# Writing out the loops over the groups on ScalarE and VectorE of a four-layer cross-attention kernel

## What is computed

```
x = L0(x, ctx)   # 1x1 convolutions over the 64 rows, both inputs normalised, attention 256 x 256
x = L1(x, ctx)   # 16 heads of 16: layer norm of ctx, Q K V, softmax, output product, times tanh(gate)
x = L2(x, ctx)   # as L1 with its own weights
x = L3(x, ctx)   # one head of 256, softmax over 64 keys, times alpha

def L1(x, ctx):  # L2 is the same
    a = layer_norm(ctx) * gamma + beta
    Q, K, V = heads(x @ Wq.T), heads(a @ Wk.T), heads(a @ Wv.T)
    p = softmax(where(mask, Q @ K.T * 0.25, -inf))
    return x + tanh(gate) * (merge(p @ V) @ Wo.T)
```

## Time and profile before

| | us |
|---|---|
| median of 3 runs | 617.71 (616.09 to 618.76) |
| the profiled execution | 619.04 |
| its span, first to last instruction | 616.9 |
| PE busy in the span | 570.0 (92%) |
| DVE busy, ACT busy | 469.0 (76%), 469.4 (76%) |
| POOL busy | 118.0 (19%) |

### The profile page before, as it was taken

The page is one execution under the profiler, slowest core; times in us unless marked ns, Lnnn a source line. Parts: engine busy times, 40 slices in busy tenths (PEclk is TensorE's granted clock), DMA queues, the critical chain, the costliest instruction groups (busy, mean ns, idle before and its releaser), DMA issues.

```text
span 616.9 us, 25805 instructions
## 1 busy us (share of the span) xinstructions
PE 570.0 (92%) x10867; PEld 502.2 (81%) x10867; DVE 469.0 (76%) x1023; ACT 469.4 (76%) x961; POOL 118.0 (19%) x132
## 2 busy tenths in 40 slices
PE   1799999999999999999999999999999999999885
PEld 1678788888888887988889887998889888998774
DVE  5785879676986879687786869778796869876553
ACT  0799878878787779867788869867788768868651
POOL 3503070103310070102500060101601051000000
PEclk9899999999999999999999999999999999999978
DMA  6420001110020100210020100210020100010001
GB/s 154 161 75 2 2 3 44 35 37 1 3 75 4 34 2 4 74 36 2 2 75 3 36 2 3 74 36 3 2 75 2 37 2 2 3 36 3 3 2 34
DMA packets 18499, 18.32 MB, mean 30 GB/s; under 512 B 1828, under 2 KB 18340, under 8 KB 18404
## 3 DMA queue, kind: packets, MB, share of 16 engines
q1 hardware_dynamic: 18024, 16.55, 8.5%
q0 software_dynamic: 320, 0.26, 0.4%
q10 hardware_dynamic: 60, 0.01, 0.0%
HBM read 12.63 MB, written 4.19 MB: 27 GB/s over the span
## 4 chain that ended last, share of the span: by engine, by line
PE 65%; DVE 15%; ACT 10%; issue 6%; DMA 1%; SPq 1%; POOL 0%; DVEq 0%; ACTq 0%; POOLq 0%
PE psum L389 10%; PE psum L731 8%; PE psum L677 8%; PE psum L391 8%; PE psum L390 8%; DVE negmax L1055 7%; PE psum L724 5%; DVE shifted L1059 4%; PE psum L641 4%; ACT work L856 3%; PE psum L656 3%; PE psum L544 3%; ACT v L807 2%; PE psum L453 2%; DMA mrow_u<-in_mask_dram 1%
## 5 line engine op out<-in xcount | busy, mean ns | idle before, releaser
L1059 DVE TENSOR_TENSOR shifted<-psum,negmax 128x512 f32<-128x512 f32 x128 | 88.5, 692 | 10.5 <-ACT work L856 5.6
L856 ACT ACTIVATE work<-shifted 128x512 f32<-128x512 f32 x128 | 79.1, 631 | 18.8 <-DVE shifted L1059 17.8
L870 ACT ACTIVATE work<-psum,group_mask 128x512 f32<-128x512 f32 x128 | 80.4, 696 | 16.4 <-PE psum L677 16.4
L1055 DVE TENSOR_REDUCE negmax<-psum 128x8 f32<-128x512 f32 x128 | 87.3, 682 | 5.9 <-PE psum L656 5.3
L677 PEld LDWEIGHTS psum<-const,work 64*128 64x128 f32 x1536 | 55.8, 141 | 33.4 <-issue 32.0
L677 PE MATMUL psum<-const,work 64*128 64x64 f32 x1536 | 65.0, 229 | 18.7 <-ACT work L856 16.6
L731 PEld LDWEIGHTS psum<-v,work 128*64 128x64 f32 x2048 | 63.9, 141 | 8.1 <-issue 5.9
L731 PE MATMUL psum<-v,work 128*64 128x34 f32 x2048 | 67.5, 227 | 0.0
L851 ACT ACTIVATE work<-psum,negmax 128x256 f32<-128x256 f32 x128 | 50.2, 511 | 12.2 <-DVE negmax L1051 12.2
L807 ACT ACTIVATE v<-psum 64x256 f32<-64x256 f32 x128 | 49.7, 388 | 10.0 <-PE psum L391 8.7
L795 ACT ACTIVATE kbd<-psum,own_bias,const 128x512 f32<-128x512 f32 x64 | 46.2, 777 | 4.8 <-PE psum L391 4.4
(11 more groups left out here) (181 smaller groups left out, 1536.1 us busy)
## 6 DMA issues: line engine op xcount, KB each, us to landing
x_raw<-in_x_dram SPq DMA_DIRECT2D x8, 512.0 KB, 4.3
c_raw<-in_ctx_dram SPq DMA_DIRECT2D x8, 512.0 KB, 5.0
out_dram<-attn SPq DMA_DIRECT2D x16, 256.0 KB, 2.3
mrow_u<-in_mask_dram SPq DMA_DIRECT2D x8, 64.0 KB, 5.1
kbd<-in_L_xattn_Wq_dram SPq DMA_DIRECT2D x2, 256.0 KB, 6.3
kbd<-in_L_xattn_Wk_dram SPq DMA_DIRECT2D x2, 256.0 KB, 6.5
kbd<-in_L_xattn_Wv_dram SPq DMA_DIRECT2D x2, 256.0 KB, 6.6
kbd<-in_L_xattn_Wo_dram SPq DMA_DIRECT2D x2, 256.0 KB, 7.1
```

The lines of the kernel that those rows point to most:

```text
L856: act.activation(probs[:, exp_row(g, l, i, last), :], shifted[:, i % 2, :], ACT.Exp).then_inc(exps, 1)
L870: act.activation(probsT[:, at, :], o[:], ACT.Copy, scale=group_mask[:, 2 * i + c:2 * i + c + 1]).then_inc(free, 1)
L1055: dve.tensor_reduce(negmax[:, i % 2, :], sv, AX_X, ALU.max, negate=True).then_inc(rowmax, 1)
L1059: dve.tensor_tensor(shifted[:, i % 2, :].rearrange("t (j k) -> t j k", k=C), sv, negmax[:, i % 2, :].unsqueeze(2).broadcast_to([P, NJ, C]) ...
```

## The change

The two loops of the chip become Python loops, so that all seven groups are written out with `g` a number. Nothing else in the file changes.

```diff
@@ scalar
-            with act.Fori(0, NG - 1) as g:
+            for g in range(NG - 1):
                 iteration(g, False)
             iteration(NG - 1, True)
@@ vector
-            with dve.Fori(0, NG - 1) as g:
+            for g in range(NG - 1):
                 iteration(g, False)
             iteration(NG - 1, True)
```

## The result

The changed kernel takes 621.12 us in the median (619.59 to 622.73, 7 runs), the kernel before, timed beside it, 618.45. The ratio is 1.0054 with a 95% interval of 1.0035 to 1.0074: slower by 0.5%, which is 3.3 us; the two medians as they stand differ by 2.7 us. The interval stays clear of 1, but its lower end lies under the 0.5% that the prediction named as the least that can be told. The forecast was 622.6 us, 4.9 us slower. The direction was right and the time lies in the range, but a third of the forecast loss did not come. The profiled execution took 621.38 us, its span is 619.4.

The account below looks back on a forecast made before the run. DVE was taken to set the time in layer 2's scores, though PE is busiest. Terms of 0.28 + 0.28 + 0.14 = 0.70 us a group, 4.9 us over seven, gave 617.7 + 4.9 = 622.6 us; range just under 619.7 to 626.0.

Parts of the forecast that it names:

- S2.0 to S2.3, four gaps: Layer 2's first four reduce-subtraction pairs on DVE: each costs 0.07 us more, all on the path to T2.0, 0.28 us a group.
- S2.4 to S2.7, four gaps: Layer 2's last four pairs on DVE, up to the release of cT.0: another 0.28 us a group.
- AT1.0 and AT1.1: DVE's attnT_lo steps after ACT's attnT_hi: PE's weight load comes 0.07 us later at each, 0.14 us a group.
- ScalarE's waits: On ACT nearly every activation carries its one wait itself in both forms; register instructions run under the activation before: 0 us.
- Mn.0, layer 1's scores, branch, L3, A1.0: Other moved waits and DVE's loop branch: 0 us, being off the path or covered by other work.
- period: The time of one group in the loop: up by 0.28 + 0.28 + 0.14 = 0.70 us.
- the stretch from S1.0 to T1.0 unchanged at 6.6 us: Layer 1's scores: moved waits cost 0 us, as the loop took 6.62 us and the written-out last group 6.61.
- A (absorbed): Layer 2: only the first half's 0.28 us reaches PE, the rest vanishes in PE's work; 619.7 us, chance 0.08.
- C (fetches): Longer DVE and ACT code: about six fetch stops of 1.1 us add 6.6 us; 629 us, chance 0.05.
- D: Nothing on the chip changes, the loop's waits being in truth as slow; 617.7 us, chance 0.03.
- B: Register instructions at L1058 hold up the waits behind them; removing them gains 4.2 us, 613.5 us; chance 0.04.

Follow-up runs that it names:

- e8: The kernel before, both loops kept, with one more POOL instruction of 128 x 200 numbers ahead of the eight normalisations L1282; 617.24 us, ratio 1.0011.
- e5: The kernel before, both loops kept, with rowmax waited for ahead of exps at the scores' subtractions; 615.07 us, ratio 0.9977.
- e9: The kernel before, both loops kept, with rowmax waited for ahead of exps and mask_set ahead of the bank at T1.0; 614.69 us, ratio 0.9961.
- e3: The changed kernel with rowmax waited for ahead of exps at the scores' subtractions (L1059, L1067); 615.12 us, ratio 0.9969 to the kernel before.
- e6: The kernel before, both loops kept, with ACT's mask_set waited for ahead of the bank at T1.0; 616.08 us, ratio 0.9999.
- e4: The changed kernel with DVE's two waits swapped at the scores and at cT/nT, Mn/Mm, AT1, AT2 and the first weighting step; 615.92 us, ratio 0.9972.
- e1: The changed kernel with ACT's loop kept, so only DVE's is written out; 621.25 us against 617.35 for the kernel before, ratio 1.0067.
- e10: The changed kernel with only the attn_hi and bank waits swapped at AT1 and AT2; one profiled execution, S1.0 to S2.0 26.66 us, 0.15 shorter.
- e2: The changed kernel with DVE's loop kept, so only ACT's is written out; 616.97 us, ratio 0.9993 to the kernel before.

## Why L990 gets shorter: e7 and e8

L990 at L.3 reads two tiles from SBUF, and POOL is at its eight normalisations L1282 at that time, one directly behind the other. What stands beside it in the changed kernel and in the kernel before (timelines of POOL and DVE):

```profile
370.63 1.21 POOL L1282 TENSOR_SCALAR x_norm<-x_raw,mean_var,rstd 128x256 f32<-128x256 f32 x1
```

```profile
368.72 1.22 POOL L1282 TENSOR_SCALAR x_norm<-x_raw,mean_var,rstd 128x256 f32<-128x256 f32 x1
```

In the changed kernel L990 starts 371.07 - 370.63 = 0.44 us behind POOL's instruction and takes 0.68. Before, it was 369.02 - 368.72 = 0.30 us and 0.79. To move nothing but this phase, e7 and e8 put one more POOL instruction ahead of the eight, of 128 x 8 numbers in e7 and 128 x 200 in e8, and keep both loops:

```diff
@@ normalise, against the kernel before; e8 has 0:200
                 hold(rstd_ready, nth)
+                pool.tensor_scalar(pool_pad[:, 0:8], x_raw[:, 0, 0:8], EPS, None, ALU.add)
                 for t in list(range(NP, 2 * NP)) + list(range(NP)):
```

> The kernel before with one POOL instruction more ahead of the eight normalisations L1282 (128 x 8 numbers into a scratch, about 0.2 us), so all eight start about 0.2 us later. In six traces VectorE's L990 at L.3 (operands in SBUF alone) lasts 681 ns plus what is missing to 410 ns from the start of the L1282 beside it: 789 to 809 ns in the kernel before, where it starts 281 to 304 ns behind, and 681 to 683 in the changed kernel, where it starts 420 to 434 ns behind. Theory (POOL holds something that L990 needs for the first 0.41 us of each L1282): L990 now starts 50 to 110 ns behind L1282 and lasts 980 to 1040 ns; the stretch from S2.0 to S2.3 grows from 6.10 to 6.30 to 6.35 us, the period by 0.2 to 0.25, the time by 1.4 to 1.7 us. Rival: L990's length has nothing to do with POOL's phase and the shorter L990 of the changed kernel comes from its being written out; then it stays at 790 to 810 ns here.

> The same with a POOL instruction of 128 x 200 numbers, about 1.0 us, ahead of the normalisations. One L1282 takes 1.20 us, so L990 at L.3 now starts about 500 ns behind the start of the L1282 beside it, beyond 410. Theory: L990 lasts 681 to 683 ns as in the changed kernel, though the loop stays, the stretch from S2.0 to S2.3 falls from 6.10 to 5.98 us, the period by about 0.1 us, the time by 0.8 us, within what can't be told. Rival as before: L990 stays at 790 to 810 ns. A second rival is that the later end of the normalisations delays PE's turning of x_norm and the period grows.

Measured: e7 617.62 us, ratio 1.0015 (0.9989 to 1.0040); e8 617.24 us, ratio 1.0011 (0.9984 to 1.0037). Both times are too small a matter to tell; the traces are not. POOL and DVE in e7 (lines are one or two higher there, L991 is the L990 of before):

```profile
370.52 1.22 POOL L1284 TENSOR_SCALAR x_norm<-x_raw,mean_var,rstd 128x256 f32<-128x256 f32 x1
```

```profile
370.62 0.99 DVE L991 TENSOR_TENSOR state_lo<-state,state_hi 128x512 fp32r<-128x512 f32 x1
```

At 0.10 us behind POOL's start the same instruction takes 0.99 us, in all seven groups (991 to 997 ns), and the period grows by 0.18 us, just under the 0.2 to 0.25 expected. That is the length that the theory forecast, with the loop in place; the rival's 790 to 810 ns falls. In e8 the phase did not become the 500 ns that I wanted, but 312 to 327, and the length is 760 to 778 ns: by the same rule (681 + 410 - 326 = 765), though the 681 to 683 ns expected were missed. The added instruction took 0.73 us and not 1.0, and the first L1282 behind it became 0.5 us longer. The second of these shows the reverse side. POOL and DVE in e8, further ahead in the same group:

```profile
361.20 1.71 POOL L1284 TENSOR_SCALAR c_norm<-c_raw,mean_var,rstd 128x256 f32<-128x256 f32 x1
```

```profile
361.12 0.68 DVE L991 TENSOR_TENSOR state_lo<-state,state_hi 128x512 fp32r<-128x512 f32 x1
```

Here L991 started 0.08 us ahead of POOL's instruction; it kept its 0.68 us, and POOL's took 1.71 instead of 1.21. Whoever comes second waits. Over all twelve traces L990 starts 78 times less than 410 ns behind the start of an L1282; start difference and duration then add up to 1085 to 1105 ns each time. In the 83 cases in which it starts later beside a running L1282, it takes 679 to 692 ns.

The Trainium skill, "SBUF — State Buffer", section "Who interferes with whom", says that a VectorE instruction with two SBUF inputs contends with a GpSimd instruction that reads SBUF; section "SBUF: two separate sides" of the same page says that whichever of the two starts first has the ports for its whole instruction and the other is blocked. On who blocks whom the traces agree, in both directions. On how long they don't: by the whole instruction L990 would have to end 1.21 + 0.68 = 1.89 us behind POOL's start, and it ends 1.09 behind it, as if POOL's share in it were over after 0.41 us of the 1.21 that the profile shows for it.

## Are the loops needed away: e5 and e9

e5 is the kernel before with e3's swap and both loops.

```diff
@@ scores_step, layers 1 and 2, against the kernel before (L3 as in e3)
+                    dve.wait_ge(rowmax, 18 * g + (8 * l - 8 + i + 1))
                     if l == 2 or i >= 2:
                         dve.wait_ge(exps, 18 * g + (8 * (l - 1) + i - 1))
-                    dve.wait_ge(rowmax, 18 * g + (8 * l - 8 + i + 1))
```

> The kernel before, loops and all, with only the two waits of L1058 (and those of the third layer at L1066) called in the other order: rowmax first, exps second. In this form a wait instruction holds exps, L1059 holds rowmax, and the register instruction carries no wait. My theory: what counts is only which instruction holds the wait that ends last, so layer 2's pairs stay at a gap of 0.03 us as in the kernel before, the period stays at 70.17 to 70.21 us, and the time is that of the kernel before within 0.3 us (the change as submitted loses, and the same reordering only repairs the written-out form). Pairs of layer 1 that wait for exps (gaps of 0.12 us in the loop, where a register instruction holds it) come to 0.10, on no path. Rival: the gain of the reordered, written-out kernel (615.1 against 617.35) comes from the reordering itself; then this one shows it too, 615 to 616 us.

Measured: 615.07 us, ratio 0.9977 (0.9957 to 0.9996). By groups it is what the theory said, 70.21 us and not one stretch moved by more than 0.02. By time it is what the rival said. My number was wrong in that I had left out the last group, which has constants in this kernel too: its eight pairs of layer 2 come down from 0.8 to 0.3 us of idle, 0.5 us for the kernel. The remaining gain of about 1 us is within the interval, and no group explains it. In the profiled execution it goes with the clock: from the last group's S1.0 to the end the kernel before has a granted clock of 0.89 in the mean and e5 of 0.92, over 65.41 us and 62.41 us. The columns are as above, the kernel before first.

```profile
551.52:616.93 65.41, 52.67 (x822) 46.48 (x818) 37.24 (x74) 35.71 (x69) 0.00 (x0) 0.89 0.05 18
551.99:614.40 62.41, 49.75 (x822) 44.21 (x818) 37.18 (x74) 35.64 (x69) 0.00 (x0) 0.92 0.06 19
```

e9 adds e6's order of waits to e5; its edit is the two diffs above together.

> The kernel before with its two loops and both reorderings of waits that the earlier runs tell apart: rowmax ahead of exps in layer 1 to 3's scores, and mask_set ahead of the bank at T1.0. Theory (the place of the wait that ends last is all that counts, the loops cost nothing): the stretch from S1.0 to S2.0 is 26.65 us, from S2.0 to S2.4 8.81, from S2.4 to S2.7 5.39 in the loop's turns, the period 70.08 to 70.13, and in the last group the eight pairs of layer 2 are 0.5 us shorter than in the kernel before. Sum against the kernel before: 7 x 0.08 + 0.5 = 1.1 us less, 615.5 to 616.5 us. Rival: the loop's form costs something that only shows when these waits are out of the way; then it is slower than the reordered written-out kernels (615.1 and 615.9 in their runs, against 617.35 for the kernel before) by more than 0.5 us relative to the kernel before.

Measured: 614.69 us against 617.29, ratio 0.9961 (0.9945 to 0.9977), with a period of 70.11 us. It has the lowest ratio of the kernels here, though its interval overlaps those of e3, e4 and e5; it is faster than the kernel before by 0.4% and than the changed one by about 0.9% (1.0054 / 0.9961, from two comparisons), with both loops in place. So in this kernel writing out brings nothing that three swapped waits don't bring as well. Its time is a little below the 615.5 to 616.5 expected; the sum of 7 x 0.08 + 0.5 = 1.1 us covers not quite half of the 2.6 us, and the interval reaches down to 1.4 us.

Part of the rest goes with the clock. In the profiled execution e9's last group takes 61.09 us at a mean granted clock of 0.96, against the 65.41 at 0.89 shown above. Every execution has its mean granted clock on record. Over the 83 executions of the kernel before that were timed beside e1 to e10, a mean clock lower by 0.01 goes with a time longer by 3.4 us (a straight line within each of the three sets). The twelve executions of e9 have 0.993 in the mean, the 17 of before beside them 0.990. Taken to the same clock by that line, an estimate, e9 gains 1.5 us (standard error 0.3) where the sum says 1.1, and e5 0.2 us (0.3) where the sum says 0.5. Whether the moved waits bring about the higher clock, or these executions had it by chance, no run shows.

## Why the prediction came out as it did

By its own steps, per group, with what was measured for each:

| step | forecast | measured | shown by |
|---|---|---|---|
| S2.0 to S2.3, four gaps | +0.28 | +0.18, about 0.28 - 0.11 of L990 | rows, e3, e7 |
| S2.4 to S2.7, four gaps | +0.28 | +0.28 | e3 |
| AT1.0 and AT1.1 | +0.14 | +0.15 | e10 |
| ScalarE's waits | 0 | -0.08 | e2, e6 |
| Mn.0, layer 1's scores, branch, L3, A1.0 | 0 | about 0 | table |
| period | +0.70 | +0.51 | |

- **The mechanism was right.** A gap of 0.03 us becomes one of 0.10 where the wait that ends last is held by a wait instruction of its own, and the last group of the trace of before was a true model of it. e3 takes the whole of it back with two swapped lines.
- **The term for S2.0 to S2.3 was mis-sized**, 0.28 for 0.18. The step that failed is "Is all of it on the path? ... 4 x 0.07 = 0.28 us". The gaps are there, but between the first and the second stands L990, whose duration I took as fixed. At this place it was 0.79 to 0.81 us in every turn of the loop and 0.68 at its other places, and the rows of before could have told: POOL was at work in that window, 3.48 us in the earlier trace rows. The added 0.07 of S2.0 and the 0.07 that the AT steps leave over shift L990 by 0.14 us against POOL's instructions, from 0.30 to 0.43 or 0.44 behind, just past the 0.41 up to which it waits. That it lands there is luck, and it holds for five of the seven groups: in g = 1 L990 starts 0.33 us behind and takes 0.76.
- **ScalarE's 0 was wrong**, by 0.08 us a group. "Nearly every activation has one wait" is true, and the one that has two sits on the path at T1.0. The sign that I gave, the stretch from S1.0 to T1.0 unchanged at 6.6 us, holds (349.48 - 342.85 = 6.63 against the 6.62 of the earlier trace rows), but it ends one instruction ahead of the place where the gain is.
- **Two errors of one sign.** 0.70 - 0.11 - 0.08 = 0.51, which is what the two periods of g = 4 give. Seven times that is 3.6 us, and 3.6 us is what the trace has up to the last group's S1.0, in part because two odd groups cancel. The groups are not all alike: the difference is 0.45 to 0.63 us in five of them, 0.02 in g = 2, where the kernel before was itself 0.5 us late at the group's end (no cause found), and 0.88 in g = 6. The last is the phase again: there L990 comes 270 and 84 ns behind POOL's start and takes 820 and 1006 ns.
- **Rivals.** A (absorbed) falls: both halves of the stretch count. C (fetches) falls: 20 packets instead of 8 on q14 (15 in e1, 14 in e2, so both engines' code is fetched there), no idle microsecond, and e3 with the same 20 packets is faster than the kernel before. D falls with the 112 wait instructions and their gaps. B is true at L869 alone, worth 7 x 0.08 = 0.6 us.

## What to carry to other kernels

Of two waits of one instruction, see to it that the one that ends last is held by the instruction itself, and not by a wait or register instruction ahead of it: each place on the path cost 0.07 to 0.08 us here, and the order of two lines decides it, in a loop and written out alike. Unrolling is no end in itself; look in the built order where each wait went. And before a duration next to an edit is taken as fixed, see whether the instruction is longer there than elsewhere in the same trace, and what another engine is doing at that time.

## What was not expected of the hardware

- DVE's L990, with both inputs in SBUF, waits for POOL's L1282 only until 0.41 us behind its start, though L1282 is shown for 1.21 us: 681 ns grow to as much as 1077 (in e10). DVE instructions that read PSUM were not longer beside L1282: L1059 took 690 to 695 ns there in the twelve traces. A step that moved by 0.14 us gained 0.11 us by this (g = 4 of the changed kernel), and one that moved by 0.19 lost 0.20 (e7).
- It is symmetric: POOL's instruction grew by 0.5 us, to 1.71, when L990 had started 0.07 to 0.08 us ahead of it (e8 in all seven groups, e4 once).
- Writing out 14 turns of two loops cost 12 packets of instruction fetch (0.16 MB for 0.07) and no stop that the trace shows.
